# Spreading the score matmuls of the levels of 32 and 64 tokens over four 32-column tiles of TensorE

## The reference, cut to what matters

```
q, k, v = silu(h @ wq), sigmoid(h @ wk), h @ wv          # 4 heads of 128
f = 1 - k;  theta = cumsum(sign(f - 0.5)) * pi           # cos/sin of it multiply q and k
S_t = S_(t-1) * f_t + k_t v_t^T;   o_t = (q_t * 256^-0.5) S_t    # a scan over 4096 tokens
out = norm(o * sigmoid(h @ wg1 @ wg2)) @ wo              # first sub-layer
out = sigmoid(xr @ W_r.T) * (relu(xk @ W_k.T)^2 @ W_v.T) # second, xr and xk mix h with the token before
```

## Time and profile before

| | us |
|---|---|
| median of 3 runs (1958.51 to 1961.96) | 1960.5 |
| the profiled execution | 1956.9 |
| its span in the profile | 1955.0 |
| busy in it: TensorE matmul | 1894.0 (97%) |
| busy: TensorE weight load | 1665.9 (85%) |
| busy: VectorE | 1464.8 (75%) |
| busy: ScalarE | 687.7 (35%) |
| busy: GpSimd | 496.1 (25%) |

### The profile page before, as it was taken

One profiled execution on the slowest core, in us unless ns is written; L12 is line 12 of the kernel. 1 busy time (PEld: TensorE's weight loads), 2 busy tenths in 40 slices (PEclk: granted clock), 3 DMA queues, 4 the chain that ended last, 5 costly groups with the idle time before them and its releaser, 6 DMA issues. The chain is left out here.

```text
span 1955.0 us, 53550 instructions
## 1 busy us (share of the span) xinstructions
PE 1894.0 (97%) x23233; PEld 1665.9 (85%) x23233; DVE 1464.8 (75%) x2900; ACT 687.7 (35%) x1279; POOL 496.1 (25%) x536
## 2 busy tenths in 40 slices
PE   5799999999999999999999999996999999999998
PEld 1688999889998999889988999885788888888887
DVE  4377677766777677767777677766899999999996
ACT  2233333333333333333333333331544344334432
POOL 2101121111111121112111121111245444544454
PEclk9899999999999999999999999998999999999999
DMA  6100011000100001000100010001211111111110
GB/s 247 65 2 24 24 32 37 24 23 24 45 24 24 23 34 35 23 23 24 46 24 23 23 40 29 24 13 50 71 65 50 60 65 65 54 55 65 65 55 33
DMA packets 42624, 84.69 MB, mean 43 GB/s; under 512 B 2308, under 2 KB 2840, under 8 KB 42392
## 3 DMA queue, kind: packets, MB, share of 16 engines
q1 hardware_dynamic: 38008, 73.42, 10.8%
q10 hardware_dynamic: 4384, 7.87, 1.1%
HBM read 47.72 MB, written 33.55 MB: 42 GB/s over the span
## 5 line engine op out<-in xcount | busy, mean ns | idle before, releaser
L148 POOL TENSOR_TENSOR ln_rs<-ln_ve,mhalf 128x2 f32<-128x2 f32 x64 | 73.5, 1149 | 986.7 <-DVE ln_ve L143 986.7
L700 DVE TENSOR_TENSOR Tot<-Tot 128x256 f32<-128x256 f32 (+2 forms) x192 | 47.2, 246 | 155.8 <-PE lvl L924 100.4
L844 PE MATMUL bank<-hT_hi,wq_hi 128*128 128x256 f32 x512 | 152.2, 297 | 10.0 <-POOL hT_lo L486 10.0
L154 DVE TENSOR_SCALAR xn<-xs,ln_mv,ln_rs 128x512 f32<-128x512 f32 x128 | 132.0, 1073 | 32.2 <-POOL ln_rs L148 32.2
L844 PE MATMUL bank<-hT_hi,wk_hi 128*128 128x256 f32 x512 | 150.4, 294 | 0.0
L792 DVE TENSOR_TENSOR og<-bank,og 128x512 f32<-128x512 f32 x64 | 44.3, 692 | 138.0 <-PE bank L1007 138.0
L844 PE MATMUL bank<-hT_lo,wq_hi 128*128 128x256 f32 x512 | 146.2, 286 | 0.0
L844 PE MATMUL bank<-hT_hi,wq_lo 128*128 128x256 f32 x512 | 146.0, 285 | 0.0
L1294 PE MATMUL bank<-xk_hi,fk_hi 128*128 128x256 f32 x512 | 144.3, 282 | 0.6 <-DVE xk_lo L1228 0.6
L844 PE MATMUL bank<-hT_lo,wk_hi 128*128 128x256 f32 x512 | 143.8, 281 | 0.0
L1294 PE MATMUL bank<-xk_hi,fk_lo 128*128 128x256 f32 x512 | 143.7, 281 | 0.0
(11 more groups left out here) (196 smaller groups left out, 5806.9 us busy)
## 6 DMA issues: line engine op xcount, KB each, us to landing
xs<-in_L_attn_x SPq DMA_DIRECT2D x32, 512.0 KB, 3.8
x_scratch<-xs SPq DMA_DIRECT2D x32, 512.0 KB, 2.9
xs<-x_scratch SPq DMA_DIRECT2D x32, 512.0 KB, 3.6
out<-xs SPq DMA_DIRECT2D x32, 512.0 KB, 2.8
mod_raw<-in_L_wmod SPq DMA_DIRECT2D x4, 1024.0 KB, 11.7
ffn_raw<-in_L_wmod SPq DMA_DIRECT2D x2, 1024.0 KB, 24.1
raw_q<-in_L_attn_wq ACTq DMA_DIRECT2D x1, 1024.0 KB, 9.5
raw_k<-in_L_attn_wk ACTq DMA_DIRECT2D x1, 1024.0 KB, 14.5
```

The lines of the kernel that those rows point to most:

```text
L148: pool.tensor_tensor(out=ln["rs"][:, :], in0=ln["ve"][:, :], in1=mhalf[:, :], op=ALU.pow).then_inc(ln["rstd"], 1)
L154: last = dve.tensor_scalar(ln["xn"][:, ch, :], chunk(ln, n, ch), ln["mv"][:, ch, 0:1], ln["rs"][:, ch:ch + 1], ALU.subtract, ALU.mult)
L700: dve.tensor_tensor(out=Tot[:, off2:off2 + cnt2], in0=t[:, :, 0], in1=t[:, :, 1], op=ALU.mult)
L844: last = pe.matmul(dst, lhs(a, s), rhs(b, s), start=(t == 0), stop=(t == len(terms) - 1))
```

## The change

The level of 32 sends the pairs with odd g one tile further (tiles 0, 2 for even g, 1, 3 for odd g), so that two g's share the 32 columns of PSUM. The level of 64 splits each matmul of 64 columns into two of 32, for c = 0 and 1, and sends c = 1 to tiles 2 and 3. ScalarE copies the level of 32 in four pieces of 32 x 128, of which the two with o = 1 go to other partitions than they come from, and the level of 64 in two of 64 x 256, of which the one with c = 1 goes from partitions 64-127 to 0-63.

```diff
                     act.wait_ge(mm["lvl"], NL * n + 6)
-                    src = level_bank(6, par)[:, 0:G * 32].rearrange("p (g t) -> p g t", g=G)
+                    src = level_bank(6, par)[:, 0:G * 16].rearrange("p (g t) -> p g t", t=32)
                     for q in range(2):
-                        last = act.copy(A[64 * q:64 * q + 32, :, 64 * q + 32:64 * q + 64], src[64 * q:64 * q + 32, :, :])
+                        for o in range(2):
+                            tile = slice(64 * q + 32 * o, 64 * q + 32 * o + 32)
+                            last = act.copy(A[64 * q:64 * q + 32, o::2, 64 * q + 32:64 * q + 64], src[tile, :, :])
                     last.then_inc(merged_act, 1)
...
                     act.wait_ge(mm["lvl"], NL * n + 7)
-                    act.copy(A[0:64, :, 64:128], level_bank(7, par).rearrange("p (g t) -> p g t", g=G)[0:64, :, :]).then_inc(merged_act, 1)
+                    src = level_bank(7, par)[:, 0:G * 32].rearrange("p (g t) -> p g t", t=32)
+                    for c in range(2):
+                        last = act.copy(A[0:64, :, 64 + 32 * c:96 + 32 * c], src[64 * c:64 * c + 64, :, :])
+                    last.then_inc(merged_act, 1)
...
                             elif m == 32:

                                 for b in (0, 2):
-                                    quad = slice(32 * b, 32 * b + 32)
-                                    last = pe.matmul(dst[quad, g * 32:(g + 1) * 32], k[:, g, quad], q[:, g, b + 1, :], start=True, stop=True)
+                                    tile = slice(32 * (b + g % 2), 32 * (b + g % 2) + 32)
+                                    last = pe.matmul(dst[tile, g // 2 * 32:g // 2 * 32 + 32], k[:, g, 32 * b:32 * b + 32], q[:, g, b + 1, :],
+                                                     start=True, stop=True)
                             else:
-                                for b in (0, 1):
-                                    quad = slice(32 * b, 32 * b + 32)
-                                    last = pe.matmul(dst[quad, g * 64:(g + 1) * 64].rearrange("p (c t) -> p c t", c=2),
-                                                     k[:, g, quad], q[:, g, 2:4, :], start=True, stop=True)
+                                for c in range(2):
+                                    for b in range(2):
+                                        tile = slice(32 * (b + 2 * c), 32 * (b + 2 * c) + 32)
+                                        last = pe.matmul(dst[tile, g * 32:g * 32 + 32], k[:, g, 32 * b:32 * b + 32], q[:, g, 2 + c, :],
+                                                         start=True, stop=True)
```

## The result

| | before | after |
|---|---|---|
| median, us | 1959.5 (4 runs, 1958.1 to 1962.0) | 1939.6 (4 runs, 1938.8 to 1941.3) |
| profiled execution, us | 1956.9 | 1939.2 |
| its span, us | 1955.0 | 1937.2 |

The ratio is 0.9898, with a 95% interval of 0.9881 to 0.9915: some 20 us faster. The page after has TensorE less busy by 17.5 us and ScalarE busier by 15.6 us, each close to the change of the span or to the copies added.

The account below looks back on a forecast made before the run. TensorE's issued stream was taken to bound the attention stage. 0.59 us a block over blocks 0 to 30 (18.3 us) plus 1.0 us in block 31 made 19.3 us, so 1941.2 us, range 1936 to 1948.

Parts of the forecast that it names:

- TensorE's stream sets the time: Attention stage: a microsecond taken from what TensorE issues is one of the kernel, until another engine falls behind.
- Level of 32: TensorE: the same 32 records, 8 on each of four tiles, save 0.24 us a block.
- Level of 64: TensorE: 64 records of 32 columns, 16 on each tile, save 0.32 us a block in place of 0.871 us.
- tail: Level of 64, last start to the next group's: 0.12 us in place of 0.15, 0.03 us saved.
- Block 31: Last block, without projections between the levels: savings scaled by its longer levels to 0.33 and 0.62, together 1.0 us.
- ScalarE at no cost: The smaller copies add 0.51 us a block, 16 us in all, to ScalarE, costed at nothing for the kernel.
- the cover that was named: ScalarE: idle 0.73 us before v_copy, then slack from g1_high to g_lo and 1.0 us on to gate_rows.
- rival 4: ScalarE: three pieces changing partitions take 1.5 us each, net 0.7 us a block slower, 1982 us; chance 3%.
- The prediction's upper bound for v_copy: ScalarE: if partition-changing pieces cost a whole copy more (0.37 us each), v_copy is 0.1 to 0.4 us late.
- Rivals 1 and 3: Level of 64: splitting gains nothing, 1952.8 us, chance 5%; or four 32-column tiles go by two, 1963.9 us, chance 3%.
- The base: Whole kernel: sum made against the profiled 1956.9 us gives 1937.6; applied to the runs' median 1960.5 it gives 1941.2 us.

Follow-up runs that it names:

- only32: The changed kernel with the level of 64 and its copy as before, so only the level of 32 is spread; 1951.3 us, ratio 0.9964.
- only64: The changed kernel with the level of 32 and its copies as before, so only the level of 64 is split and spread; 1946.7 us, ratio 0.9938.
- split_two: The changed kernel with the level of 64 split into 64 records of 32 columns, all on tiles 0 and 1; 1955.6 us, ratio 0.9985.
- whole_four: The changed kernel with the level of 64 unsplit, 32 records of 64 columns, odd g on tiles 2 and 3; 1936.5 us, ratio 0.9889.
- even_odd: whole_four with g issued in the order 0, 2, 4, 6, 1, 3, 5, 7 at the level of 64; 1944.3 us, ratio 0.9933.
- by_twos: whole_four with g issued in the order 0, 2, 1, 3, 4, 6, 5, 7 at the level of 64; 1937.6 us, ratio 0.9897.
- act_plus4: The changed kernel with 4 small ScalarE copies (8 columns) ahead of each of the two levels' copies; 1939.7 us, ratio 0.9910.
- act_plus14: The changed kernel with 14 small ScalarE copies (8 columns) ahead of each of the two levels' copies; 1941.0 us, ratio 0.9914.
- act_plus45: The changed kernel with 45 small ScalarE copies (2 columns) ahead of each of the two levels' copies; 2039.0 us, ratio 1.0411.
- the second comparison: The unmodified changed kernel run again on another chip, beside the kernel before; 1939.6 us, ratio 0.9906.

## Why the prediction held

- **TensorE's stream sets the time.** Right. No recurring wait came, and each change of a group's time was found in the period, which fell from 39.79 us (966.06 to 1005.85) to 39.19 (953.60 to 992.79), 0.60 where 0.59 was forecast. The other kernels say the same (groups to the next group and median periods, in us below the kernel before):

| | both groups | period |
|---|---|---|
| only32 | 0.24 | 0.27 |
| only64 | 0.32 | 0.36 |
| split_two | 0.12 | 0.13 |
| the change | 0.56 | 0.60 |
| whole_four | 0.67 | 0.71 |
| even_odd | 0.43 | 0.46 |

- **Level of 32.** 0.24 forecast. 0.62 to 0.39 in these rows (0.628 to 0.388 in the median), and only32 shows it alone.
- **Level of 64.** 0.32 and 0.03 of tail forecast, so 0.35; 1.02 to 0.69 is 0.33 (0.324 in the median). It is the row with 64 records on four tiles that gave the right price: (0.76 - 0.196) / 16 is 35 ns, and 33 for the level of 32, (0.46 - 0.196) / 8.
- **The rest of the period.** 0.24 and 0.33 leave 0.03 us. It lies in places the prediction didn't speak of, first of all between the levels of 2 and 4 (the last row of each pair is cut off by the end of its view, so its count is below 64):

```profile
971.41 0.39 PE L844 MATMUL bank<-hT_hi,wq_hi 128*128 128x256 f32 x1
...
974.48 0.69 PE L924 MATMUL lvl<-Q,K 128*32 128x16 f32 x60
```
(the kernel before) and, in the changed one,

```profile
958.94 0.38 PE L849 MATMUL bank<-hT_hi,wq_hi 128*128 128x256 f32 x1
...
961.96 0.62 PE L929 MATMUL lvl<-Q,K 128*32 128x16 f32 x52
```
  From the first projection to the start of the next level, the same 24 projections take 3.07 us before and 3.02 after; 0.02 us of that is lost again in front of the level of 32 (2.98 to 3.00). The spread of neither level brings it: only32 and only64 each show all of it, which is why their periods fall by 0.63 us together and the change's by 0.60, and by_twos, which has both levels spread, takes 3.07 us again. What brings it is open. It is part of the 0.60 and no part of the reasons given, so that the 0.60 meets the 0.59 is in part luck: the two groups alone give 0.56.
- **Block 31.** 1.0 us forecast, none found in the profiled executions, where both need 631 us from the last `near` on. This term failed. Its two groups did get shorter:

```profile
1323.88 0.46 PE L935 MATMUL lvl<-Q,K 128*32 128x32 f32 x32 [1.51 <-DVE K L719]
...
1325.85 1.08 PE L941 MATMUL lvl<-Q,K 128*32 128x32 f32 x64 [1.51 <-DVE K L719]
```
  (0.98 and 1.92 us before), which is 1.4 us. But the clock took it back ahead of them. These are 4 us at the same distance behind the first start of `near` in block 31, before and after:

```profile
1329.90:1333.90 4.00, 4.00 (x79) 1.00 0.02 6
```
```profile
1312.00:1316.00 4.00, 4.00 (x42) 0.57 0.04 9
```
  The level of 32 starts 16.9 us behind that `near` before (1340.19 - 1323.28) and 18.5 after (1323.88 - 1305.42), 1.6 us later. Both executions have 17 us at the lower level from that `near` to the end of the stage, but after, some of it fell here, where TensorE is busy without a pause, and not among its waits for VectorE. I had scaled two durations by the clock that they happened to meet, but where the clock falls around the end of the stage moves from execution to execution. In act_plus4's profiled execution its stretches at the lower level were as before in number and length (one of 10.2 us around the two levels, then two of 3.4), and from the first start of that `near` on it took 630.6 us against 631.7 before: about the 1.0 us forecast. That is one execution and suggests the term's mechanism, no more.
- **ScalarE at no cost.** Right. The pieces cost 0.26 and 0.37 us, as worked out, and the cover that was named is the one that act_plus14 used up in part and act_plus45 in full. The order of rival 4 (idle, then g_lo, then gate_rows) is right; its price left out the clock. The prediction's upper bound for v_copy is mis-summed: two pieces at 0.37 us more each would end the copies at 989.61, 0.6 us late and not 0.1 to 0.4. Nothing hangs on it, as no piece cost more.
- **Rivals 1 and 3.** split_two refutes both directly. Rival 1 leaned on a rule of the Trainium skill, "TensorEngine Tiling (Array Packing)", section "Instruction Overhead": some 60 cycles for every matmul, one column as much as 60. Read in columns, as the prediction did, it doesn't hold here: a record of 32 columns costs its tile 32 to 35 ns, one of 48 costs 43 and one of 64 costs 54. Read in cycles it isn't refuted. 54 ns for 64 columns is 0.84 ns a column, two cycles of 2.4 GHz; 60 cycles would be 25 ns, an estimate from the page's figure, and a floor does show here, at 32 to 35 ns for 16 and 32 columns alike. The rule's advice not to split a small dimension is right here too, by whole_four: 32 columns stand at the floor already, so half of 64 costs more than half.
- **The base.** The profile's 1956.9 against a median of 1960.5 led to 1941.2; the runs gave 1939.6, a gain of 19.9 where 19.3 was the sum. How close that is says little: the two profiled executions lie 17.7 us apart, the second comparison gave 18.1, and the interval of the ratio spans 17 to 23 us. The firm figure is the period, 31 x 0.60 = 18.6 us.

## What to carry to other kernels

Where a busy engine sets the time, price a group of small matmuls by its time to the next group and divide by the records on each tile; here that forecast 0.59 us a block, of which the two groups gave 0.56. Spread narrow outputs over all four column tiles by an index that exists anyway, such as the head or chunk, instead of cutting the moving operand, and let the tiles alternate in the order of issue. An engine that is idle for half of the time has only as much room as lies in its chain up to the next reader: here 3 us of a 39 us block.

## What was not expected of the hardware

- TensorE started matmuls on idle column tiles ahead of earlier ones that waited for a busy tile (even_odd), but only a few records ahead: 0.83 us for a run of 16, 0.61 for runs of 8, 0.58 for runs of 4.
- A copy of 2 or 8 columns from PSUM adds 0.06 us to ScalarE's queue, a copy of 128 columns 0.26.
- Waits of TensorE, one in each of 31 blocks, of 2.1 to 2.2 us (the first 4.8), cost more than the idle time counted for them: 69.5 us of idle time made 99 us. 74 are the waits from start to start, and about 18 are the granted clock, which fell to 0.50 for 3.4 us behind 11 of them.
